# Gate, up and key-value products in split operands, a new opening and middle, and expert tails in pairs

## The reference

```
mod = silu(c) @ wmod            # six vectors of 256 per batch: sa, ca, ga, sb, cb, gb
h = layernorm(x) * (1 + ca) + sa
fused = h @ w_kv_a              # 320 columns: q latent 192, kv latent 64, k_pe 64
q = rmsnorm(q_c) @ w_qb; kv = rmsnorm(kv_c) @ w_kvb      # 16 heads
scores = q_full . k_full * scale, causal; probs = softmax(scores)
x = x + ga * ((probs @ v) @ w_o)
h = layernorm(x) * (1 + cb) + sb
top 4 of 16 experts per token from softmax(h @ gate_w.T), first 128 tokens per expert kept
y = sum over experts of weight * (silu(h @ w_gate) * (h @ w_up)) @ w_down   # inner width 176
shared = (silu(h @ sw_gate) * (h @ sw_up)) @ sw_down                        # inner width 352
x = x + gb * (y + shared)
```

## Time and profile before

| what | value |
|---|---|
| three runs | 1292.52, 1293.26, 1293.86 us; median 1293.26 |
| profiled execution | 1287.12 us, of which the profile's span is 1285.3 us |
| PE busy, TensorE clock granted (mean) | 93% of the span, 0.966 of full speed |
| DVE, ACT, POOL busy | 66%, 52%, 22% |
| one batch | 140 us: eight pairs of about 12.2 us and a middle of about 41 us |
| experts, first add to last landing | 1206.9 to 1283.6 us |

### The profile page before, as it was taken

The page is one execution under the profiler, slowest core; times in us unless marked ns, Lnnn a source line. Parts: engine busy times, 40 slices in busy tenths (PEclk is TensorE's granted clock), DMA queues, the critical chain, the costliest instruction groups (busy, mean ns, idle before and its releaser), DMA issues.

```text
span 1285.3 us, 25913 instructions
## 1 busy us (share of the span) xinstructions
PE 1193.3 (93%) x7556; PEld 954.7 (74%) x7556; DVE 848.6 (66%) x2579; ACT 667.5 (52%) x1922; POOL 279.6 (22%) x332
## 2 busy tenths in 40 slices
PE   6699999999999999999999999999999999995874
PEld 4488877887688768887788768886888768882542
DVE  3367757776687668775777668766877677756221
ACT  1367634675367626764477526762577346741220
POOL 1000022211322132212221122113212132202553
PEclk8799999999999999999999999999999999998985
DMA  9510002000010001000100001000100000003762
GB/s 305 139 45 0 0 1 65 3 0 0 16 49 0 0 16 49 0 0 0 45 20 0 0 16 49 0 0 16 49 0 0 0 30 20 0 1 100 213 150 37
DMA packets 48317, 46.17 MB, mean 36 GB/s; under 512 B 10048, under 2 KB 44960, under 8 KB 48296
## 3 DMA queue, kind: packets, MB, share of 16 engines
q1 hardware_dynamic: 29096, 30.90, 8.3%
q0 software_dynamic: 7168, 6.37, 2.8%
q10 hardware_dynamic: 12032, 8.65, 2.3%
HBM read 35.04 MB, written 15.11 MB: 39 GB/s over the span
## 4 chain that ended last, share of the span: by engine, by line
PE 78%; DVE 9%; DMA 5%; issue 3%; ACT 2%; POOL 2%; POOLq 0%; DVEq 0%; SPq 0%; ACTq 0%
PE PS L675 11%; PE PS L696 10%; PE PS L654 7%; PE PS L655 6%; PE PS L656 6%; PE PS L797 6%; DMA out<-x_res,toku 5%; PE PS L640 5%; PE PS L805 3%; PE PS L827 3%; PE PS L788 2%; PE PS L627 2%; PE PS L630 2%; PE PS L631 2%; PE PS L628 2%
## 5 line engine op out<-in xcount | busy, mean ns | idle before, releaser
L973 ACT ACTIVATE probs<-probs,nmax 128x512 f32<-128x512 f32 (+3 forms) x512 | 283.1, 554 | 127.0 <-DVE nmax L1229 123.1
L1229 DVE CUSTOM_DVE_ANT_0 probs<-PS,cmask 128x512 f32<-128x512 f32 (+3 forms) x512 | 229.3, 488 | 101.0 <-PE PS L656 97.9
L538 POOL DMA_INDIRECT tab_dram<-entry,slot x112 | 110.5, 986 | 389.9 <-PE PS L696 368.6
L654 PE MATMUL PS<-kTh,qTh 128*128 128x512 f32 (+3 forms) x512 | 176.9, 345 | 0.6 <-DVE qTl L1260 0.6
L982 ACT ACTIVATE pT<-PS 128x384 f32<-128x384 f32 (+3 forms) x320 | 126.8, 462 | 77.9 <-PE PS L675 77.9
L675 PE MATMUL PS<-ident,probs 128*128 128x128 f32 x1280 | 165.7, 276 | 0.0
L656 PE MATMUL PS<-kTh,qTl 128*128 128x512 f32 (+3 forms) x512 | 165.4, 323 | 0.0
L655 PE MATMUL PS<-kTl,qTh 128*128 128x512 f32 (+3 forms) x512 | 165.4, 323 | 0.0
L696 PE MATMUL PS<-pT,kmat 128*64 128x512 f32 (+3 forms) x1024 | 152.0, 439 | 0.3 <-issue 0.3
L675 PEld LDWEIGHTS PS<-ident,probs 128*128 128x128 f32 x1280 | 142.4, 141 | 10.3 <-issue 7.4
L696 PEld LDWEIGHTS PS<-pT,kmat 128*64 128x64 f32 x1024 | 68.0, 136 | 76.0 <-issue 62.1
(11 more groups left out here) (237 smaller groups left out, 2112.8 us busy)
## 6 DMA issues: line engine op xcount, KB each, us to landing
x_in<-in_x SPq DMA_DIRECT2D x8, 512.0 KB, 5.9
modb<-mod_dram SPq DMA_DIRECT2D x8, 512.0 KB, 5.4
h_dram<-mod_dram SPq DMA_DIRECT2D x1, 4096.0 KB
h_dram<-h SPq DMA_DIRECT2D x8, 512.0 KB, 3.0
out<-base SPq DMA_DIRECT2D x8, 512.0 KB
pT<-in_wo SPq DMA_DIRECT2D x1, 2048.0 KB, 11.7
tab_dram<-entry,slot POOLq DMA_INDIRECT x112
oT<-in_wqnT SPq DMA_DIRECT2D x1, 1536.0 KB, 10.2
```

What stands on the lines that cost most here:

```text
L538: pool.indirect_dma_start(tab_dram[:, :], bass.IndirectOffsetOnAxis(ap=slot[:, j:j + 1], axis=0), entry[:, j, :], None, bounds_check=NE * ...
L654: pe.matmul(PS[:, bank, 0:n], qTh[:, h, rows_q], kTh[:, 0:n], start=True, stop=False)
L973: act.activation(probs[:, UO[u]:UO[u] + UW[u]], probs[:, UO[u]:UO[u] + UW[u]], ACT.Exp, scale=-1.0, bias=nmax[:, u:u + 1], accum_out=psums ...
L1229: dve.tensor_tensor_reduce(out=probs[:, UO[u]:UO[u] + UW[u]], in0=PS[:, SBANK[u], 0:UW[u]], in1=cmask[:, S - UW[u]:S], scale=-1.0, scalar= ...
```

## The change

**Split operands.** `hT` and `h2T` become `hTh` and `hTl`, and the weights of the key-value, gate, up and router products become high and low parts. Each of these products is three rounded ones in place of one plain f32 product. For an activation ACT now writes two copies out of PSUM, one full (into `tmp`) and one rounded; DVE subtracts them (`h1_low`, `h2_low`). `h2_low` reads two tiles in SBUF. The router's product is divided in two: 384 token columns first (`ffn_router(b, 0, ...)`), and 128 columns when token tile 3 is there.

**Middle.** POOL's scaling of `h2` also waits for `rope_ready` now, that is for the DVE instruction that writes the first query tile of the next batch. The first transposes of `h1` go ahead of the last pair's transposes of probabilities.

**Opening.** The activations of batch 0 are turned first, `absorb_query(1)` goes behind the key-value product, and `absorb_output` behind the first query product. The shared expert's weights are loaded later and split by ACT and DVE behind the first pair; PE waits for both there.

**Tail.** The last batch's tokens are seated by rank among the four choices, with 16 one-hot tiles in place of 64. Experts are added to the output in pairs: PE turns the token numbers (`turn_tokens`), DVE finds which tokens stand in both experts of a pair (`same_tokens`), PE's `merge(k)` moves their results from the odd expert to the even one, DVE adds (`merge_out`), and POOL issues both adds of a pair together. The inner width is divided as 88 + 88 rows in place of 128 + 48.

```diff
                 pool.wait_ge(h2T_ps, 3 * (b + 1))
+                if n is not None:
+                    wait_alone(pool, rope_ready, n * NPAIR + 1)
                 pool.tensor_tensor(h2[:], h2[:], spread(2), ALU.mult).then_inc(h2_scaled, 1)
...
+            def scatter_add(e, index):
+
+                pool.indirect_dma_start(outr, bass.IndirectOffsetOnAxis(ap=index, axis=0), ey[e % NT], None,
+                                        bounds_check=T - 1, oob_is_err=False, compute_op=ALU.add).then_inc(added, 16)
+
             pool.wait_ge(base_out, B * 16 + 16)
-            for e in range(NE):
-                pool.wait_ge(ey_ready, e + 1)
-                if e:
-                    pool.wait_ge(added, 16 * e)
-                pool.indirect_dma_start(outr, bass.IndirectOffsetOnAxis(ap=toku[:, e:e + 1], axis=0),
-                                        ey[e % NT], None, bounds_check=T - 1, oob_is_err=False,
-                                        compute_op=ALU.add).then_inc(added, 16)
-                if e + ROWS_AHEAD < NE:
-                    gather_rows(e + ROWS_AHEAD)
+            for k in range(NE // 2):
+                pool.wait_ge(merged_ready, k + 1)
+                if k:
+                    pool.wait_ge(added, 32 * k)
+                scatter_add(2 * k + 1, destu[:, k:k + 1])
+                scatter_add(2 * k, toku[:, 2 * k:2 * k + 1])
+                for e in (2 * k + ROWS_AHEAD, 2 * k + 1 + ROWS_AHEAD):
+                    if e < NE:
+                        gather_rows(e)
...
                     pe.wait_ge(gated_ready, 2 * b - 1)
+                if last and more:
+                    turn_h1(b + 1, 0, 6)
                 turn_probs(g, first, (0, 1))
                 if not last:
                     q_turn(g + 1)
                 elif more:
-                    turn_h1(b + 1, 0)
-                turn_probs(g, first, (2, 3))
-                if last and more:
-                    turn_h1(b + 1, 1)
-                turn_probs(g, first, (4, 5))
+                    turn_h1(b + 1, 1, 6)
+                turn_probs(g, first, (2, 3, 4, 5))
...
+                gate, up, m = PS[0:w, banks[0], :], PS[0:w, banks[1], :], slice(off, off + w)
                 for c in range(2):
-                    if m == 2:
-                        pe.wait_ge(h2T_ready, 4 * b + c + 3)
-                    pe.matmul(PS[0:wide, banks[0], :], sg_sb[:, c, off:off + wide], h2T[:, c, :],
-                              start=c == 0, stop=c == 1)
-                    mm = pe.matmul(PS[0:w, banks[1], :], su_sb[:, c, off:off + w], h2T[:, c, :],
-                                   start=c == 0, stop=c == 1)
+                    pe.matmul(gate, sg_h[:, c, m], hTh[:, c, :], start=c == 0, stop=False)
+                    pe.matmul(gate, sg_l[:, c, m], hTh[:, c, :], start=False, stop=False)
+                    pe.matmul(gate, sg_h[:, c, m], hTl[:, c, :], start=False, stop=c == 1)
+                    pe.matmul(up, su_h[:, c, m], hTh[:, c, :], start=c == 0, stop=False)
+                    pe.matmul(up, su_l[:, c, m], hTh[:, c, :], start=False, stop=False)
+                    mm = pe.matmul(up, su_h[:, c, m], hTl[:, c, :], start=False, stop=c == 1)
                 mm.then_inc(gu_ps, 1)
+
+            def ffn_router(b, part, banks):
+
+                off, w = MT[2]
+                cols = slice(0, S - P) if part == 0 else slice(S - P, S)
+                gate, up = PS[0:w + NE, banks[0], cols], PS[0:w, banks[1], cols]
+                mg, mu = slice(off, off + w + NE), slice(off, off + w)
+                for c in range(2):
+                    pe.wait_ge(h2T_ready, 4 * b + 2 * part + c + 1)
+                    pe.matmul(gate, sg_h[:, c, mg], hTh[:, c, cols], start=c == 0, stop=False)
+                    pe.matmul(gate, sg_l[:, c, mg], hTh[:, c, cols], start=False, stop=False)
+                    pe.matmul(up, su_h[:, c, mu], hTh[:, c, cols], start=c == 0, stop=False)
+                    pe.matmul(up, su_l[:, c, mu], hTh[:, c, cols], start=False, stop=False)
+                pe.wait_ge(h2Tl_ready, 2 * b + part + 1)
+                for c in range(2):
+                    pe.matmul(gate, sg_h[:, c, mg], hTl[:, c, cols], start=False, stop=c == 1)
+                    mm = pe.matmul(up, su_h[:, c, mu], hTl[:, c, cols], start=False, stop=c == 1)
+                return mm
 
...
                         for c in range(2):
-                            mm = pe.matmul(PS[:, t, 0:FW], hT[:, c, bass.ts(t, P)], wkva_sb[:, c, :],
-                                           start=c == 0, stop=c == 1)
+                            pe.matmul(PS[:, t, 0:FW], hTh[:, c, bass.ts(t, P)], wkva_h[:, c, :],
+                                      start=c == 0, stop=False)
+                            pe.matmul(PS[:, t, 0:FW], hTh[:, c, bass.ts(t, P)], wkva_l[:, c, :],
+                                      start=False, stop=False)
+                        if k == 0:
+                            pe.wait_ge(hTl_ready, 2 * (n + 1))
+                        for c in range(2):
+                            mm = pe.matmul(PS[:, t, 0:FW], hTl[:, c, bass.ts(t, P)], wkva_h[:, c, :],
+                                           start=False, stop=c == 1)
                         mm.then_inc(kv_ps, 1)
...
                     q_project(0, n * NPAIR, (2, 3))
+                if not post:
+                    absorb_output()
                 if post:
+                    pe.wait_ge(x1_ready, 3 * b + 3)
+                    ffn_router(b, 0, (3, 4))
                     pe.wait_ge(n2_ready, 2 * b + 2)
                     turn_h2_last()
-                    ffn(b, 2, (3, 4))
+                    ffn_router(b, 1, (3, 4)).then_inc(gu_ps, 1)
                 if pre:
...
+            turn_h1(0, 0, 6)
+            turn_h1(0, 1, 7)
+            pe.wait_ge(wq_in, 3 * 16)
+            absorb_query(0, range(0, NH // 2))
+            turn_modulation()
+            absorb_query(0, range(NH // 2, NH)).then_inc(wabs_ps, 1)
             middle(0, 0, False, True)
             step(0, 0, True, False, False)
+            pe.wait_ge(ffnh_ready, 1)
+            pe.wait_ge(ffnl_ready, 1)
...
+            def merge(k):
+                pe.wait_ge(ey_ready, 2 * k + 2)
+                if k:
+                    pe.wait_ge(merged_ready, k)
+                pe.matmul(PS[:, 5, 0:H], same[:, k, :], ey[(2 * k + 1) % NT],
+                          start=True, stop=True).then_inc(merge_ps, 1)
+
+            turn_tokens()
             turn_rows(0)
             for e in range(NE):
                 gate_up(e)
@@ -942,9 +1028,13 @@
                     turn_rows(e + 1)
                 if e >= 2:
                     down(e - 2)
+                if e >= 4 and e % 2 == 0:
+                    merge(e // 2 - 2)
             turn_inner(NE - 1)
             down(NE - 2)
+            merge(NE // 2 - 2)
             down(NE - 1)
+            merge(NE // 2 - 1)
 
...
+                for c in parts:
                     act.wait_ge(hT_ps, 2 * n + c + 1)
-                    act.activation(hT[:, c, :], PS[:, 6, :], ACT.Identity, scale=mod1[:, 2 + c:3 + c],
+                    act.activation(h1_full[:, c, :], PS[:, bank, :], ACT.Identity,
+                                   scale=mod1[:, 2 + c:3 + c], bias=mod1[:, c:c + 1])
+                    act.activation(hTh[:, c, :], PS[:, bank, :], ACT.Identity, scale=mod1[:, 2 + c:3 + c],
                                    bias=mod1[:, c:c + 1]).then_inc(hT_ready, 1)
...
+            act.wait_ge(init_out, 6 * 16)
+            act.activation(sg_h[:], sg_st, ACT.Copy)
+            act.activation(su_h[:], su_st, ACT.Copy).then_inc(ffnh_ready, 1)
...
                 group_out(g, 3)
+                if last and more:
+                    h1_low(b + 1)
                 group_out(g, 5)
...
                     normed(x1, h2, mv2, rstd2, range(3, 4), n2_ready)
+                    h2_low(b, 0, slice(0, S - P))
                 if pre:
                     for part in q_rope(n * NPAIR):
                         part()
+                if post:
+                    h2_low(b, 1, slice(S - P, S))
...
+            def h1_low(n):
+
+                for c in range(2):
+                    dve.wait_ge(hT_ready, 2 * n + c + 1)
+                    dve.tensor_tensor(hTl[:, c, :], h1_full[:, c, :], hTh[:, c, :].bitcast(F32),
+                                      ALU.subtract).then_inc(hTl_ready, 1)
+
+            def h2_low(b, part, cols):
+
+                dve.wait_ge(h2T_ready, 4 * b + 2 * part + 2)
+                dve.tensor_tensor(hTl[:, :, cols], h2_full[part], hTh[:, :, cols].bitcast(F32),
+                                  ALU.subtract).then_inc(h2Tl_ready, 1)
+
+            def query_low(k):
...
+            dve.wait_ge(ffnh_ready, 1)
+            dve.tensor_tensor(sg_l[:], sg_st, sg_h[:].bitcast(F32), ALU.subtract)
+            dve.tensor_tensor(su_l[:], su_st, su_h[:].bitcast(F32), ALU.subtract).then_inc(ffnl_ready, 1)
...
                 if e >= NT:
```

(27 more changed lines are left out.)

281 lines of the change are left out of this document (176 added, 105 removed).

## The result

The changed kernel takes 1312.78 us (median of four runs, 1309.18 to 1315.25) against 1293.22 for the kernel before on the same chip: 1.0149 times as long, with a 95% interval of 1.0124 to 1.0174. Its profiled execution took 1309.18 us with a span of 1307.3, 22.0 above the span before.

What follows compares the result with a forecast made beforehand. PE carries 78% of the last-ending chain, while POOL's adds pace the last stage. Terms +28 (expert pairs), -1 (middles), +1 (opening) sum to +28 on a 1287.1 us profile, plus 6 to the median: 1320, range 1299 to 1331.

Steps and rivals of the forecast that it cites:

- Pairs of experts, +28 at the end: Tail: five gather-bound rounds of 16 us, then 7.4 and 6.5; end at 1313.3 against 1285.3, +28.
- rival (a): Tail: adds alone set the pace, seven distances of 7.4 us if rows lie ready; 1279 us, chance 0.10.
- First add at 1212: Tail: first add needs merge(0), two turns later; 1206.9 - 1.6 + 6.7 = 1212 us.
- the seating: Last batch's seating: -3.8 us up to the shared expert's last product; the first expert's product 1.6 us earlier.
- Half clock behind the wait: Expert rounds: PE stands some 7 us, then halved clock: down 2.14, gate_up 2.5; up to 17 a round, 16 taken.
- Rival (b): Tail: expert rounds at full clock, 13.6 us each, 12 us less; 1308 us, chance 0.17.
- Opening, +1: Opening: -8 earlier query product, +0.8 absorb_output, +5.7 weight wait, +3.3 low clock: +1.8; bounds -4 and +5, +1 taken.
- Middles, -0.1 each: Each middle with a next batch: +0.6 key-value path, +0.6 port stall, -1.2 rounded products; about 0, say -0.1.
- From batch 0 to the rank product: Seven middles after the opening: -1 in all, bounds -14 and +15.
- The port's stall: Middle: h2_low(b, 1) stopped by POOL's instruction until 334.5; PE reaches q_turn at 335.1 against 334.47, +0.6.
- rival (c): Middles: no stall at the port, seven middles at -2.0; 1307 us, chance 0.12.
- The difference between profile and median: Whole kernel: median of runs 6 us above the profiled execution, as in the kernel before; result rounded to 1320.

Runs made afterwards that it cites:

- the last experiment: Merge ahead of turn_rows and down, against the changed kernel with rows eight ahead, GpSimd's h2 scaling later, low shared weights on GpSimd: 1242.29 us, 0.9671 of the kernel before.
- the second run of the changed kernel: The changed kernel unaltered, measured again on the chip of the next three experiments: 1316.14 us, 1.0206 of the kernel before.

## Why the prediction came out right

The forecast was slower, at 1320; it is 1312.8, inside the range of 1299 to 1331 and just under the forecast's own (1313 to 1328). The term that decides, the rounds held by the gathers, is right by its mechanism. That the rest of the sum fits is partly luck: the forecast has the opening 4.7 us too long and what follows, up to the last batch's rank product, 3.9 too short, and the two nearly cancel. Point by point:

- *Pairs of experts, +28 at the end.* Right in mechanism: adds in pairs, five rounds held by the gathers and two not. The round was put at 16 and is 15.4, which is 3 us of the 6 between 1313.3 and the real end at 1307.3. With rows two rounds earlier it is 7.4 to 8.7, about as rival (a) has it; what was not met here is its condition. Its 7.4 holds the merge too, and the adds alone need 6.6, by the last experiment.
- *First add at 1212.* It is 1208.92, the other 3 us. From the first `gate_up` to the first add 15.1 us pass for 9.0 before, +6.1 for a forecast of 6.7. The mis-sized term is the seating: from the rank product to the first expert's product it saves 3.3 us and not 1.6, for the weight loads, which I had let hold that product, hold nothing. A further 0.8 is that the rank product itself comes early.
- *Half clock behind the wait*. Right, with `down` at 1.06 us as in the rows before, and `gate_up` at 2.55, which had 2.71 there. It ends within the round, so the round is 15.4 and not 17. Rival (b), full clock at 13.6, is out.
- *Opening, +1.* The parts: the first query product 10.4 us earlier, not 8; the wait 5.47 for a forecast of 5.7; the half clock behind it 2.3 at the most (the run with the low weights on GpSimd), not 3.3. At the last value products of batch 0, behind eight pairs, the changed kernel is at 154.30 where the kernel before is at 158.03: -3.7. So the sum of +1 has the wrong sign, and the opening lies near its lower bound of -4.
- *Middles, -0.1 each.* At full clock this is right: +0.1 for the one in the windows above. The key-value product starts 1.35 us later against the last pair, for a forecast of 1.6, and its own length saves 0.6 and not 1.0. The forecast put the later start down to ACT's copies; the run without the copy of h1 gives back only 0.65, and PE's wait for the norm in front of the first transposes was in no term. The gain of 1.2 + 1.0 on the products is 2.2 by the run with plain ones.
- *From batch 0 to the rank product.* Seven middles were to give -1. From -3.7 at the last value products of batch 0 to -0.8 at the rank product the difference grows by 2.9. The first middle, which has the half clock, holds 1.6 of it (the next token load is at 217.93 for 220.02), the next five none, and the rest lies behind the last load.
- *The port's stall.* At full clock it was sized right. Its absence was to be worth 1.9 a middle, rival (c), and the run that takes it away gives 1.8. But it gives 21 us in all beside the second run of the changed kernel, because the half clock goes with it. That part was missing from every case: it lifts the later runs of the changed kernel above the first profile.
- *The difference between profile and median.* I put 6 us on it, the difference of the kernel before; it is 3.6.

**What held at the port.** L1314 alone takes 0.69, L1656 alone 0.42 us, and 1.96 beside GpSimd's L522. The rule of the Trainium skill, "SBUF — State Buffer", section "Who interferes with whom", that a VectorE instruction with two SBUF inputs contends with a GpSimd one that reads SBUF, and that the holder keeps the shared pair for its whole instruction, agrees in the main: L1656 ends at 332.76, and L522, which began 0.67 ahead of it, at 332.48. So 0.28 of its 0.42 us lie behind the other's end.

## What to carry to other kernels

When work is grouped to save round trips, look at what is issued behind the group: a prefetch that was one step ahead of its use can fall behind it, and here one constant was worth 36.6 us of the experts' rounds. When a helper engine is moved out from beside one instruction, ask which instruction it stands beside now, and move it behind the last one that the critical engine waits for. Price a wait of the matrix engine at its length and at the half clock that may follow.

## What was not expected of the hardware

- A wait of 1.4 us behind one of 0.9 is followed by up to 5 us at half clock in some middles and in others of the same execution by none (0.43 us between rounded products of 512 columns, or 0.23). With the 1.4 gone, none of the seven middles shows it, in four runs. The kernel before waits 0.86, 0.55 and 1.32 us in this stage and has none either. What decides isn't settled.
- Three rounded products of 512 columns cost 0.70 us and a plain one 0.86, so the split product is the shorter, though it has three instructions for one.
- GpSimd making the low halves (two instructions, 3.42 us) beside a pair of heads cost PE nothing: the window's clock is 1.00 and PE is busy for 22.95 of 25 us. But only one VectorE instruction with two SBUF inputs met them, the rope's last, 0.25 us before the end of the second, and it took 0.80 us for 0.69. So this doesn't show that such work is free at another place.
